# A square moved from ScalarE to GpSimd, and blank rows written behind each expert's tokens instead of under them

## The reference

```python
# third: a scan over each of 4 sequences of 1024 tokens, 256 hidden channels
delta = softplus(xa @ Wdelta.T + bdelta)
A_bar = exp(delta * A)
B_bar = delta * (xa @ Wb.T + bb)
A_cum = cumprod(A_bar, axis=1)
h_st = cumsum(B_bar / A_cum, axis=1) * A_cum
out_ssm = h_st @ Wc.T + bc + (xa @ Wd.T + bd)
x_res = silu(out_ssm @ W2.T)
out = out_ssm + (out_ssm * x_res) @ Wlast.T
# fourth: 8 experts, top 2 of the router; of the two, the later expert's output stands
for i in range(E):
    wi = w_flat[:, i:i + 1]
    h = relu((x_flat * wi) @ w1[i].T + b1[i])
    y = h @ w2[i].T + b2[i]
    out = where(wi > 0, y, out)
```

## Time and profile before

| | |
|---|---|
| three runs | 1731.05, 1735.71, 1740.53 us; median 1735.71 |
| profiled execution | 1735.71 us, span 1733.9 us |
| mean granted TensorE clock | 0.941 |
| busy: PE, DVE, ACT, POOL | 1542.6 (89%), 1308.7 (75%), 1298.2 (75%), 518.4 us (30%) |
| DMA | 84.83 MB, 49 GB/s |

### The profile page before, as it was taken

The page is one execution under the profiler, slowest core; times in us unless marked ns, Lnnn a source line. Parts: engine busy times, 40 slices in busy tenths (PEclk is TensorE's granted clock), DMA queues, the critical chain, the costliest instruction groups (busy, mean ns, idle before and its releaser), DMA issues. The chain is left out here.

```text
span 1733.9 us, 38769 instructions
## 1 busy us (share of the span) xinstructions
PE 1542.6 (89%) x13958; PEld 836.8 (48%) x13958; DVE 1308.7 (75%) x1885; ACT 1298.2 (75%) x2481; POOL 518.4 (30%) x741
## 2 busy tenths in 40 slices
PE   5999999999987999999999999998899965763397
PEld 4555555555553444343434444346677721223287
DVE  2777777777759999999999999954645546875475
ACT  2777777777763899989989989986688758863187
POOL 0222222222236100101011011205799902333466
PEclk8999999999995999999999999998999987886599
DMA  2121123232204010011001100005244300003221
GB/s 75 30 84 60 56 73 107 90 121 77 85 19 115 28 31 16 4 20 31 8 4 31 33 5 26 17 1 102 49 99 87 60 16 0 1 0 139 57 66 32
DMA packets 49388, 84.83 MB, mean 49 GB/s; under 512 B 19232, under 2 KB 25128, under 8 KB 48752
## 3 DMA queue, kind: packets, MB, share of 16 engines
q1 hardware_dynamic: 43888, 76.25, 16.6%
q0 software_dynamic: 5376, 6.96, 1.5%
HBM read 32.78 MB, written 23.92 MB: 33 GB/s over the span
## 5 line engine op out<-in xcount | busy, mean ns | idle before, releaser
L1050 ACT ACTIVATE m_probs<-m_ring 128x512 f32<-128x512 f32 x1024 | 543.2, 598 | 77.0 <-PE m_ring L966 61.3
L1129 DVE TENSOR_REDUCE m_half_max<-m_pairs 128x2 f32<-128x1024 f32 x512 | 588.0, 1216 | 11.6 <-PE m_pairs L949 11.1
L436 DVE TENSOR_REDUCE a_neg_max<-a_scores 128x1 f32<-128x1024 f32 x257 | 310.5, 1215 | 91.4 <-PE a_scores L363 91.4
L424 ACT ACTIVATE a_probs<-a_scores,a_neg_max 128x1024 f32<-128x1024 f32 x256 | 285.4, 1115 | 124.1 <-DVE a_neg_max L436 124.1
L981 PE MATMUL m_acc<-m_probs,m_v_aug 128*32 128x256 f32 (+1 forms) x4032 | 326.4, 396 | 0.0
L966 PE MATMUL m_ring<-m_q_max,m_k 32*128 32x512 f32 x1024 | 318.1, 498 | 4.0 <-DVE m_q_max L1143 3.0
L949 PE MATMUL m_pairs<-m_k,m_q 32*128 32x512 f32 x1024 | 263.6, 512 | 13.4 <-DVE m_half_max L1129 9.6
L363 PE MATMUL a_scores<-a_q,a_k_own 64*128 64x512 f32 x516 | 261.0, 622 | 6.5 <-ACT a_probs L424 5.6
L363 PE MATMUL a_scores<-a_q,a_k_other 64*128 64x512 f32 x516 | 259.4, 622 | 0.5
L966 PEld LDWEIGHTS m_ring<-m_q_max,m_k 32*128 32x128 f32 x1024 | 146.5, 183 | 217.2 <-ACT m_probs L1050 111.6
L472 POOL TENSOR_TENSOR a_scaled<-values,a_inv 128x128 f32<-128x128 f32 x256 | 102.0, 399 | 366.4 <-DVE a_inv L454 235.5
(11 more groups left out here) (283 smaller groups left out, 2116.8 us busy)
## 6 DMA issues: line engine op xcount, KB each, us to landing
sorted_tokens<-a_blank SPq DMA_DIRECT2D x8, 2176.0 KB
e_gates<-sorted_results SPq DMA_DIRECT2D x64, 256.0 KB, 8.4
a_k_other<-a_k_own SPq DMA_DIRECT2D x66, 128.0 KB, 2.3
m_k<-m_k_init SPq DMA_DIRECT2D x8, 512.0 KB, 6.6
m_q<-xT SPq DMA_DIRECT2D x8, 512.0 KB, 7.4
f_records<-sorted_tokens SPq DMA_DIRECT2D x40, 68.0 KB, 1.8
e_w<-e_w_dram SPq DMA_DIRECT2D x1, 2064.0 KB, 7.9
xT<-x_t_dram SPq DMA_DIRECT2D x1, 2048.0 KB, 7.8
```

What stands on the lines that cost most here:

```text
L424: nc.scalar.activation(probs[:, g, :], scores[:, slot(h * G + g), :], ACT.Exp, bias=neg_max[:, g:g + 1], accum_out=total[:, g:g + 1]).then ...
L436: nc.vector.tensor_reduce(neg_max[:, i % G:i % G + 1], scores[:, slot(i), :], AX, ALU.max, negate=True).then_inc(max_done, 1)
L1050: nc.scalar.activation(probs[:, u % SLOTS, head, :], ring[:, bank, :], ACT.Exp, scale=0.5).then_inc(ring_taken, 1)
L1129: nc.vector.tensor_reduce(half_max[:, pair // PAIRS % 2, at:at + 2], pairs[:, pair % 2, :, :], AX, ALU.max).then_inc(pair_taken, 1)
```

## The change

The square q moves from ScalarE's `square` to a tensor_tensor on POOL, behind z of the same step. The fills of the scratch regions leave the first attention stage, with their tile, their row numbers' input and their semaphores. In their place the routing stage makes 16 blank tiles on POOL; SyncE writes the 8 unused tiles at once, and, when `start` is known, 128 blank rows behind each expert's last record. The first record loads wait for these writes too.

```diff
@@ first_attention_stage, sync
-                def rows_of(e):
-                    sp.wait_ge(blank_zero, 1)
-                    if e:
-                        sp.wait_ge(filled, 32 * e)
-                    sp.dma_start(blank[:, :, D:].bitcast(U32), blank_rows[:, e, :, :]).then_inc(blank_rows_in, 16)
-                def fill(e):
...
-                    sp.dma_start(scratch[at:at + N, :].rearrange("(c p j) d -> p c (j d)", p=D, j=BLANK_ROWS),
-                                 all_rows.unsqueeze(1).broadcast_to(wide)).then_inc(filled, 16)
-                    sp.dma_start(scratch[at + N:at + REGION, :].rearrange("(p j) d -> p (j d)", j=BLANK_ROWS),
-                                 all_rows[0:TILE // BLANK_ROWS, :]).then_inc(filled, 16)
...
-                    else:
-                        e, at = divmod(head - len(loads), 2)
-                        if e <= E:
-                            if at == 0:
-                                rows_of(e)
-                            else:
-                                fill(e)
-                sp.wait_ge(filled, 16 * (2 * E + 1))
@@ first_attention_stage, gpsimd
-                nc.gpsimd.memset(blank[:, :, :], 0.0).then_inc(blank_zero, 1)
@@ scan_stage, scalar
                 def square(k):
-                    act.wait_ge(z_done, k + 1)
-                    if k >= 3:
-                        act.wait_ge(quad_done, k - 2)
-                    nc.scalar.activation(q[:, k % 3, :], z[:, k % 4, :], ACT.Square).then_inc(q_done, 1)
                     act.wait_ge(q_done, k + 1)
@@ scan_stage, gpsimd, ratio(k)
                     nc.gpsimd.tensor_tensor(z[:, k % 4, :], u[:, k % 3, :], inverse[:, k % 3, :],
                                             ALU.mult).then_inc(z_done, 1)
+                    pool.wait_ge(z_done, k + 1)
+                    if k >= 3:
+                        pool.wait_ge(squared_done, k - 2)
+                        pool.wait_ge(quad_done, k - 2)
+                    nc.gpsimd.tensor_tensor(q[:, k % 3, :], z[:, k % 4, :], z[:, k % 4, :], ALU.mult).then_inc(q_done, 1)
@@ place_stage, sync
+                sp.wait_ge(blank_set, 1)
+                last = E * REGION + (SORT_TILES - UNUSED) * TILE
+                sp.dma_start(scratch[last:last + UNUSED * TILE, :].rearrange("(t p) d -> p t d", p=TILE),
+                             blank[:, E:, :]).then_inc(padded_done, 16)
+                sp.wait_ge(pads_known, 1)
+                for e in range(E):
+                    at = sp.value_load(pad_at[0:1, e:e + 1], min_val=0, max_val=E * REGION)
+                    sp.dma_start(scratch[ds(at, TILE), :], blank[:, e, :]).then_inc(padded_done, 16)
                 sp.wait_ge(table_made, 1)
                 first = [sp.value_load(tile_base[0:1, t:t + 1], min_val=0, max_val=E * REGION + (SORT_TILES - 1) * TILE)
                          for t in range(PER)]
+                sp.wait_ge(padded_done, 16 * (E + 1))
                 sp.wait_ge(scattered, 16 * TILES)
@@ place_stage, vector, table()
+                    then(nc.vector.tensor_copy(pad_at[0:1, :], start[0:1, :]))
+                    dve.sem_inc(pads_known, 1)
@@ place_stage, gpsimd
+                nc.gpsimd.memset(blank[:, :, :], 0.0).then_inc(blank_zero, 1)
+                pool.wait_ge(blank_zero, 1)
+                pool.wait_ge(order_in, 16)
+                nc.gpsimd.tensor_copy(blank[:, :, D + 1].bitcast(U32), rows_of_out[:, TILES:]).then_inc(blank_set, 1)
```

More of the change, by code:

```diff
@@ L26 @@
 E = 8
[L29 to L38, removed]
 class Core:
@@ L223, in _, with first_attention_stage @@
                                          ACT.Copy).then_inc(copied, 1)
-def first_attention_stage(core, xT, y, w_q, w_k, values, loads, scratch, blank_rows):
+def first_attention_stage(core, xT, y, w_q, w_k, values, loads):
     nc = core.nc
@@ L266, in first_attention_stage @@
         loaded = core.sem("a_loaded")
[L267 to L270, removed]
         CREDIT = G
@@ L1884, in _ @@
                         gate(b)
+SORT_TILES = (N + E * (TILE - 1)) // TILE + 1
+SORT_TILES += -SORT_TILES % 4
+TABLE = SORT_TILES + 2
 PER = BANK // D
+REGION = N + TILE
+UNUSED = 8
+RECORD = D + 8
+DUMP = E + UNUSED
+U32 = mybir.dt.uint32
+I32 = mybir.dt.int32
 def place_stage(core, src, mean_w, ident, router, order, records, scratch, tile_expert, tile_base, loads, sorted_records,
@@ L1910, in place_stage @@
     at = D + E * (PER_BATCH + 1)
-    tile_rows, rows_of_out = order[:, at:at + TABLE], order[:, at + TABLE:at + TABLE + TILES]
-    at += TABLE + TILES
+    tile_rows, rows_of_out = order[:, at:at + TABLE], order[:, at + TABLE:at + TABLE + TILES + DUMP]
+    at += TABLE + TILES + DUMP
     region, earlier_first = order[:, at:at + E], order[:, at + E:at + 2 * E]
@@ L1920, in place_stage @@
         eps = core.sb("p_eps", [D, 1], F32, st)
+        blank = core.sb("p_blank", [TILE, DUMP, RECORD], F32, st)
+        pad_at = core.sb("p_pad_at", [1, E], I32, st)
         turned = core.ps("p_turned", [TILE, 2, BANKS, BANK], st)
@@ L1961, in place_stage @@
         recorded = core.sem("p_recorded")
+        blank_zero = core.sem("p_blank_zero")
+        blank_set = core.sem("p_blank_set")
+        pads_known = core.sem("p_pads_known")
         table_made = core.sem("p_table_made")
+        padded_done = core.sem("p_padded_done")
         scattered = core.sem("p_scattered")
@@ L2171, in _ @@
                 dve.wait_ge(order_in, 16)
-                nc.vector.tensor_copy(records[:, :, D + 1].bitcast(U32), rows_of_out).then_inc(recorded, 1)
+                nc.vector.tensor_copy(records[:, :, D + 1].bitcast(U32), rows_of_out[:, 0:TILES]).then_inc(recorded, 1)
                 then(nc.vector.tensor_copy(counts[:, :, 0], region))
@@ L2490, in build @@
                     constants.append((tiles.q[0][:, g, :].bitcast(F32), xT[:, PAD + N:PAD + N + S]))
-                first_attention_stage(core, xT, y, w_q, w_k, values, constants, scratch, a["blank_rows"])
+                first_attention_stage(core, xT, y, w_q, w_k, values, constants)
             tiles.add(core, st)
@@ L2606, in layouts @@
         np.broadcast_to(np.arange(TABLE) * TILE, (D, TABLE)),
-        row[:, None] + TILE * np.arange(TILES),
+        row[:, None] + TILE * np.arange(TILES + DUMP),
         np.broadcast_to(np.arange(E) * REGION, (D, E)),
         np.broadcast_to(np.arange(E, 0, -1) / 16, (D, E))], axis=1).astype(np.float32)
-    behind_end = N + (row[:, None] * BLANK_ROWS + np.arange(BLANK_ROWS))
-    blank_rows = np.zeros((D, E + 1, BLANK_ROWS, RECORD - D), np.uint32)
-    for e in range(E):
-        blank_rows[:, e, :, 1] = N + TILE * e + (behind_end - N) % TILE
-    blank_rows[:, E, :, 1] = behind_end + TILE * E
     def of_channels(v):
@@ L2633, in layouts @@
         "s_w": np.ascontiguousarray(s_w.transpose(2, 0, 1)),
-        "blank_rows": blank_rows,
         "s_vecs": np.ascontiguousarray(s_vecs),
```

## The result

The changed kernel takes 1747.06 us, the median of 20 runs (1739.60 to 1757.48); the kernel before took 1737.21 over 20 runs beside it (1731.05 to 1746.08). The ratio is 1.0064, with a 95% interval of 1.0049 to 1.0080. The predicted 1742.0 is 5 us short; the time lies in the range of 1731 to 1752. On the scale of the prediction it is "slower by over 0.5%", to which it gave 0.41, and not the likeliest "within 0.5%", though the interval reaches down to 1.0049.

A forecast was written before the change was run, and what follows sets the result against it. TensorE was busiest overall, but in the scan stage ScalarE and VectorE took turns, with VectorE and POOL sharing a port. Scan stage +14.3 − 8 = +6.3, attention and routing 0: 1735.7 + 6.3 = 1742.0 us, range 1731 to 1752.

The forecast's parts named there:

- +14.3 and −8: Scan stage: VectorE loses 14.3 us to POOL's reads and gets 8 us of its waits back, together +6.3 us.
- The 4 us of waits to be left: Scan stage: of 11.5 us of VectorE's waits some 4 stay, about 1.3 in each of three places.
- the price of the port: Scan stage: POOL and two-SBUF-input VectorE instructions share a way into SBUF and run in turn; 1.01 us per POOL op.
- 13.1 for q's and 1.2 for z's: Scan stage: 13 of 16 q's cost VectorE 1.01 us each; z's cost about 0.3 more in some four steps.
- The hand-made step: Scan stage: one worked-out step after the change; z costs quad about 0.4, q costs front 1.06, period 4.96 us.
- The signs named beforehand: Scan stage: q 1.27 undisturbed, fronts or log1ps about 1.7 in nearly each step, log1p's mean over 1.1, last scans 6.3 later.
- 1.12 us apiece, so eight take 9.0: Routing stage: SyncE's eight pads, priced like the next stage's record loads, take 9.0 us, to 1621.6.
- margin of 2.0 us: Routing stage: SyncE's four register loads end at 1624.1, 2.0 us ahead of 1626.2, when SyncE goes on; cost 0.
- 0.4 us slower: Routing stage: if each pad write issued 0.4 us slower, 3.2 in all, the cost would be +1.1 us.
- The dear port: Rival, scan stage: q's cost 1.07 each, more z's block, only 4 us come back; +14.3, 1750 us; chance 0.25.
- the relief that wins: Rival, scan stage: q's mean price under 0.5 us, so the stage gets faster; −6.7, 1729 us; chance 0.10.
- The routing stage moves: Rival, routing stage: POOL's 5.34 us wait goes, 1737 us, or the pads run late by 3, 1745; chance 0.15.

The follow-up runs named there:

- square_only: The kernel before with only the square q moved from ScalarE to POOL; ratio 1.0006 (0.9984 to 1.0028) to the kernel before.
- padding_only: The kernel before with only the padding moved, q still on ScalarE; ratio 1.0052 (1.0029 to 1.0075) to the kernel before.
- q_write_only: The changed kernel with POOL's multiply for q replaced by writes of a spare tile and a constant, reading nothing; 1739.30 us, run once.
- pads_few: padding_only's kernel with five pads on ScalarE's queue, three on SyncE's, register loads without bounds; ratio 1.0003 (0.9977 to 1.0029) to the kernel before.
- pads_split: Padding by eight dynamic writes, q on ScalarE, with four pads sent from SyncE's queue and four from ScalarE's; 1743.17 us, run once.
- static_pads: The kernel before, fills kept, plus the changed kernel's padding with its eight pads at fixed addresses, one instruction each; 1728.52 us, run once.
- pads_after_scatters: Padding by eight dynamic writes, q on ScalarE, with SyncE waiting for all of POOL's scatters before the first pad; 1746.53 us, run once.
- pads_by_act: The changed kernel with the eight pads' register loads and writes moved from SyncE's to ScalarE's queue; ratio 1.0066 (1.0034 to 1.0097) to the kernel before.

## Why the prediction was right in range and wrong in its parts

**The scan stage: right sign and mechanism, +6.3 predicted, +3.7 (+3.0 in square_only).** From first size to last scans VectorE's busy time (the third) rose from 84.72 to 96.94, by 12.2, and what is left of the stretch, its waits, fell from 19.2 to 10.7, by 8.5; together the +3.7.

```profile
1438.85:1542.75 103.90, 68.07 (x114) 24.82 (x113) 84.72 (x95) 91.32 (x142) 35.94 (x21) 0.82 0.00 0
...
1443.22:1550.81 107.59, 71.29 (x114) 25.77 (x113) 96.94 (x94) 81.81 (x126) 61.71 (x37) 0.78 0.00 0
```

The sum had +14.3 and −8. By instructions, taking quad and log1p of before from the earlier trace rows and front from padding_only's equal row (13.1 us),

```profile
L1777 DVE SCALAR_TENSOR_TENSOR d_front<-d_squared,d_z 128x512 f32<-128x512 f32 x16 | 13.1, 821 | 0.0
```

front rose by 7.3, quad by 4.0 and log1p by 0.7, and the scans, which the sum left out, by 1.3 (22.0 to 23.3 for the eight); that this is 13.3 and not 12.2 is overlap of neighbours. The waits fell by 11.1 at quad, rose by 2.6 at front and stayed at log1p. The 4 us of waits to be left were 2.6, in three places, the longest 1.3, as predicted. So the mis-sized term is the price of the port, and inside it the split was wrong: it had 13.1 for q's and 1.2 for z's. In q_write_only, where only the z's block, the three VectorE groups sum to 43.9, 6.2 more than before (37.7); with q they sum to 49.7. As far as that kernel stands for the changed one, the z's grew dearer by 6.2, as they no longer fall into VectorE's waits, and q's cost 5.8 (the rest of the 8.2 is in the scans, 21.9 and 23.3 us, and in front's waits, 1.5 and 2.6), since a front that waits for q starts at a point where part of q is over: it loses 0.83 (1.52 − 0.69), not 1.06. The hand-made step has the right shape: quad was to lose 0.4 and the front all of q; the step shown has 0.8 and 0.83, and quads lose 0.3 in three other steps. Its period of 4.96 compares with 5.16 (front at 1459.28 and 1464.44).

**The signs named beforehand.** Fronts at 1.5 were there in 8 of the 16 steps, not in nearly each, and two more at 1.75 as before; the group mean of front rose to 1.28. That of log1p did not go over 1.1; it is 0.86, as z and q mostly meet quad and front (four log1ps take 1.34). And q on POOL takes 1.37 in most steps and 1.04 in the first, not 1.27.

**The attention stage: 0 predicted, 0 measured.** Four heads at 56.66, and 507.81 against 508.02 at its end; and pads_few, without the fills, is at 1.0003 of the kernel before (0.9977 to 1.0029).

**The routing stage: 0 predicted, bounds 0 and +3; +7.3 measured.** This step failed: "1.12 us apiece, so eight take 9.0". The 1.12 came from record loads in the expert stage. There POOL scatters nothing until 1647.36, and then one scatter in about 2.2 us, with other work between; beside those 20 loads still took 22.98 us, 1.15 each. So a scatter now and then does no harm, and a row of the same instructions, taken beside the wrong neighbours, looked safe. The pads stand beside the last eight or nine scatters, where SyncE got through 21 instructions from 1621.4 to 1634.8, 0.64 us each, and they have 48. The prediction's margin of 2.0 us is worth three of those. Its own mark of failure, SyncE's first record load waiting behind the pads, is what the profile shows. The bound for this, "0.4 us slower" for each write, looked at the wrong unit. A sign was perhaps in the trace of before, unread: with the first row of 16 scatters under way or just over, VectorE stood idle 2.67 us ahead of an instruction at 1599.64, and ScalarE 4.98 ahead of one at 1597.50, in the middle of a series of equal activations. That this is the same slowness no run here shows. The four register loads of the earlier trace rows, at full speed beside the scatters, spoke against it, and they were too few instructions to tell.

**The memset on POOL** cost nothing: padding_only's first scatter comes no later in the stage, and its time is all in the pads.

**The rivals.** The dear port (+14.3) and the relief that wins (−6.7) did not come: the scan moved by 3 to 4. "The routing stage moves" came, with "the pads run late" at 7.3 and not 3; the wait of 5.34 us on POOL stayed (5.40). 1735.7 + 3.7 + 7.3 is 1746.7, beside 1747.06 measured; the 1735.71 of before that the sum started from is itself 1.5 under the median of 20. The forecast was too high by 2.6 in one place and too low by 7.3 in the other, so that 5 us off in all flatters it.

## What to carry to other kernels

Cost a moved piece of queue work by its instructions, register loads and assertions included, and take their duration from a row that has the same neighbours: eight writes known beforehand are 8 instructions, eight at run-time addresses were 48. When a helper engine is to relieve another, ask whether its instructions read SBUF beside two-input instructions of VectorE: here the relief was worth 3.5 to 4.5 us and the reads cost 8. And relief has a second bill, for transfers or instructions of others that used to fall into waits that are now gone, as the z's did. And a difference of 1.7 us in a stretch that no edit touches came with the clock: look at the granted clock there before reading anything into it.

## What the runs showed of the hardware that I had not expected

- While POOL issues a row of indirect scatters one after the other (0.96 us each, 0.30 apart), SyncE's and ScalarE's queues slow down to about one instruction each 0.70 us, whatever it is: register operation, assertion, move or DMA. In the runs read here it begins 9 to 15 us after the row's first scatter (changed kernel: 1612.18 and 1621.4; ScalarE in pads_split: 1608.12 and 1620.0; static_pads latest: 1597.29 and 1612.0), after 4 to 17 quick instructions of the queue in question; SyncE's queue was given nothing before, so that an earlier start would not have been seen. It is over 2.4 to 2.7 us after the end of the last scatter (1628.02 and 1630.5; 1632.10 and 1634.8). Without scatters it is gone (pads_after_scatters), and beside scatters 2.2 us apart in the expert stage as well (1.15 us for six instructions). With 16 of 48 instructions left out the pads are through 2.9 us sooner (13.6 and 16.5). Why is open: the DMA engines were under a quarter busy.
- The Trainium skill calls the cost of crossing into an engine's next block of instructions mostly hidden (Runtime: NRT & Kernel Launch, "Instruction fetch mechanics"). That these 0.70 us are a fetch held up by the scatters is a guess that would fit a stock of quick instructions; no run here shows it, and the instruction queues had no packet in the stretch.
- Two profiled executions whose work up to the scan stage is the same reached it 9.5 us apart (padding_only 1437.15, pads_by_act 1446.69). A difference of spans must be cut into stages before it says anything about a change of this size.
